# A fused attention and top-1 expert layer: the router's logits by small products from the attention output and the normalised x

## The reference

```python
x = x + tanh(g_xattn) * attention(layernorm(x), ctx, ctx, mask, ...)   # ends in  @ W_o.T + b_o
x = x + tanh(g_ffn) * experts(layernorm(x), gate_w, w1, w2)

def experts(tokens, gate_w, w1, w2):
    gate_logits = tokens @ gate_w.T                  # 2048 x 16
    probs = softmax(gate_logits)
    top1 = argmax(gate_logits)
    mask = one_hot(top1)
    ranks = cumsum(mask, axis=0) - 1
    mask = mask * (ranks < capacity)                 # capacity 160
    ...                                              # every token's row goes to its expert's place
    h = gelu(dispatch @ w1);  expert_out = h @ w2
    out = probs of the chosen expert * expert_out, back in the token's place
```

## Time and profile before

| | |
|---|---|
| median of 3 runs | 346.85 us (345.79 to 347.67) |
| the profiled execution, its own time | 344.49 us |
| its span | 342.7 us |
| TensorE busy | 313.1 us (91%) |
| VectorE busy | 203.1 us (59%) |
| ScalarE busy | 172.8 us (50%) |
| GpSimd busy | 148.6 us (43%) |
| granted TensorE clock, mean | 0.984 |

### The profile page before, as it was taken

How to read it: one execution, slowest core, us unless ns; L and a number is a source line. 1 busy time by engine, 2 the same in 40 slices (tenths; PEclk the granted TensorE clock), 3 DMA queues, 4 the chain that set the end, 5 groups by cost and what they waited for, 6 DMA issues and landing times.

```text
span 342.7 us, 8453 instructions
## 1 busy us (share of the span) xinstructions
PE 313.1 (91%) x2820; PEld 250.7 (73%) x2820; DVE 203.1 (59%) x974; ACT 172.8 (50%) x650; POOL 148.6 (43%) x179
## 2 busy tenths in 40 slices
PE   8868979989989897998879999999999999999990
PEld 4436756876678764886648888888888888888870
DVE  2799788999989895999953333222333333333221
ACT  2489999998999886999302111111111111111110
POOL 6479476676696637665444121222222222111122
PEclk9998999999999999899999999999999999999997
DMA  7911595139621303030053798998988888888300
GB/s 219 297 41 24 197 374 141 26 74 383 215 104 24 95 3 123 7 113 0 2 188 136 215 325 283 292 297 268 275 266 277 271 273 269 261 267 285 130 17 12
DMA packets 42070, 60.54 MB, mean 177 GB/s; under 512 B 3704, under 2 KB 32912, under 8 KB 42032
## 3 DMA queue, kind: packets, MB, share of 16 engines
q1 hardware_dynamic: 38928, 53.28, 49.2%
q0 software_dynamic: 2560, 6.25, 5.1%
q10 hardware_dynamic: 544, 0.52, 0.4%
HBM read 44.60 MB, written 14.19 MB: 172 GB/s over the span
## 4 chain that ended last, share of the span: by engine, by line
PE 60%; DVE 14%; ACT 13%; issue 7%; POOL 3%; POOLq 0%; DVEq 0%
PE bank L1586 20%; PE bank L1603 16%; ACT probs L629 10%; PE bank L1613 4%; DVE probs L827 4%; PE bank L1285 3%; PE bank L1254 2%; DVE rows L894 2%; PE bank L1232 2%; POOL expert_queue L496 2%; DVE probsT L846 2%; PE bank L1193 2%; PE bank L1243 2%; ACT q_par L603 2%; PE bank L1273 1%
## 5 line engine op out<-in xcount | busy, mean ns | idle before, releaser
L629 ACT ACTIVATE probs<-probs,low 128x128 f32<-128x128 f32 x256 | 99.1, 400 | 1.9 <-DVE low L827 1.9
L757 ACT ACTIVATE w_raw<-bank 128x480 f32<-128x480 f32 (+1 forms) x48 | 25.2, 526 | 122.9 <-PE bank L1586 122.9
L480 POOL TENSOR_TENSOR probs<-probs,r_total 128x512 f32<-128x512 f32 x64 | 66.4, 1052 | 31.9 <-DVE r_total L836 31.8
L1586 PE MATMUL bank<-xdT,w 128*128 128x160 f32 x512 | 75.1, 300 | 0.7 <-DVE xdT L1146 0.7
L1586 PEld LDWEIGHTS bank<-xdT,w 128*128 128x128 f32 x512 | 71.6, 190 | 1.7 <-issue 0.9
L1159 DVE SCALAR_TENSOR_TENSOR base<-bank,base 32x256 f32<-32x256 f32 x64 | 30.6, 477 | 65.3 <-PE bank L1613 63.7
L560 POOL DMA_INDIRECT out_dram<-base,place x16 | 15.6, 977 | 116.2 <-DVE base L1167 109.4
L1603 PE MATMUL bank<-w,w_raw 128*128 128x256 f32 x256 | 62.1, 385 | 0.0
L827 DVE CUSTOM_DVE_ANT_0 probs<-bank,mask_now 128x128 f32<-128x128 f32 x256 | 57.3, 284 | 4.4 <-PE bank L1273 4.0
L1603 PEld LDWEIGHTS bank<-w,w_raw 128*128 128x128 f32 x256 | 46.5, 190 | 11.1 <-issue 6.2
L629 ACT ACTIVATION_READ_ACCUMULATOR probs<-probs,low 128x1 f32 x256 | 51.2, 200 | 0.0
(11 more groups left out here) (123 smaller groups left out, 411.1 us busy)
## 6 DMA issues: line engine op xcount, KB each, us to landing
w<-in_L_ffn_w_dram SPq DMA_DIRECT2D x32, 1024.0 KB, 6.2
expert_queue<-empty_row SPq DMA_DIRECT2D x1, 5140.0 KB, 18.2
q_rows<-expert_queue SPq DMA_DIRECT2D x16, 160.0 KB, 6.2
base<-expert_queue SPq DMA_DIRECT2D x16, 129.0 KB, 5.5
ctx_rows<-in_ctx_dram SPq DMA_DIRECT2D x4, 512.0 KB, 10.0
out_dram<-rows SPq DMA_DIRECT2D x4, 512.0 KB, 4.1
x_all<-in_x_dram SPq DMA_DIRECT2D x3, 512.0 KB, 7.2
v_shift<-v SPq DMA_DIRECT2D x12, 128.0 KB, 2.3
```

The source lines that it names most:

```text
L480: pool.tensor_tensor(probs[:, i % NP_], probs[:, i % NP_], r_total[:, i % NP_].unsqueeze(2).to_broadcast([P, PAIRS, 2 * WINDOW]), ALU.mult ...
L629: last = act.activation(probs[:, i % NP_, j], probs[:, i % NP_, j], ACT.Exp, scale=-1.0, bias=low[:, i % NP_, j:j + 1], accum_out=total[:, ...
L757: act.activation(hidden[:, ms[0]:ms[-1] + 1, :], ps_hidden[m][:, 0:n].rearrange("p (m c) -> p m c", c=CAP), ACT.Gelu_apprx_tanh).then_inc( ...
L1586: last = pe.matmul(ps_hidden[m][:, c * CAP:(c + 1) * CAP], w1_sb[i % 2][:, k, f * P:(f + 1) * P], xdT[i % 2][:, k], start=(k == 0), stop=( ...
```

## The change

It uses that layernorm only shifts and scales: x1n times the gate is (x1 times the gate with its row mean taken off) times x1's reciprocal deviation. Maximum and one-hot don't need the positive factor. And x1 is x plus tanh(g) times (attention output times W_o + b_o), so that

- `gate_parts`, once: W_o times the centred gate (`gate_att`, 6 products in all) and b_o times it (`gate_bias`);
- `x_gate`, per batch: the gate times the turned normalised x, 8 products with 32 columns standing, into four strips of ps_wide; `take_x_gate` (VectorE copy 128x128), `x_gate_turn` (one transpose), `x_logits_of` (VectorE, times std, the reciprocal of rstd), `base_logits` (GpSimd adds gate_bias);
- `att_gate` the same with attT and gate_att, `take_att_gate`, `att_gate_turn`, and `sum_logits` (VectorE) the sum of both; `choose` reads that;
- `scale_logits` (GpSimd) multiplies the lowered logits by x1's reciprocal deviation, and `exp_logits` waits for it;
- `x1nT_of`, both `take_x1nT` and `route` of batches 0 to 2 are gone. In the last batch `route` multiplies attT by gate_att directly.

Other things that the same diff moves: a batch's four scatters stand in four places among the norms and reach into the next batch; the last batch's pieces are tiles 0 to 2 and tile 3, x1 of it is made in three parts, and its last eight units go through the windows in another order (both head groups of windows 4, 5 and then of 6, 7), so that tile 2 is complete after chunk 2; expert 0's queued rows are loaded early with batches 0 and 1 alone, and batch 2 goes through `dispatch` too; all 22 `keep_warm` products of the last batch and the tail are gone; W_o is turned later in batch 0; the weights of expert 1 are loaded in batch 2 instead of 1; and the written-out orders of the last batch are new on every engine.

```diff
+            def gate_parts(ps):
+                pe.wait_ge(wT_taken[4], 1)
...
+                for g in range(KD):
+                    for d in range(KD):
+                        pe.matmul(ps[:, g * QUARTER:(g + 1) * QUARTER], w_raw[:, 3, d, g * P:(g + 1) * P], gateT[:, d],
+                                  start=(d == 0), stop=(d == KD - 1))
...
+            def x_gate(n, ps):
...
+                for k in range(KD):
+                    for t in range(T):
+                        last = pe.matmul(ps[t * QUARTER:(t + 1) * QUARTER, 0:P], gateT[:, k], xnT[:, k, t * P:(t + 1) * P],
+                                         start=(k == 0), stop=(k == KD - 1))
+                last.then_inc(x_gate_ready, 1)
...
+            def att_gate_turn(n, ps):
+                pe.wait_ge(att_gate_taken, n + 1)
+                pe.transpose(ps[:, P:2 * P], att_logitsT[:], ident[:]).then_inc(logits_ready, 1)
...
+            def sum_logits(n, ps):
...
+                dve.wait_ge(logits_ready, n + 1)
+                dve.wait_ge(x_logits_based, n + 1)
+                dve.tensor_tensor(logits[:], ps[:, P:2 * P].rearrange("p (t e) -> p t e", e=QUARTER)[:, :, 0:E],
+                                  x_logits[n % 2][:], ALU.add).then_inc(logits_summed, 1)
...
+            def scale_logits(n, m=0):
...
+                pool.tensor_tensor(scaled[:, ts], lowered[:, ts],
+                                   rstd2[:, n % 2, ts].unsqueeze(2).to_broadcast([P, len(tiles(n, m)), E]), ALU.mult
+                                   ).then_inc(scaled_ready, 1)
```

TensorE in batches 1 and 2 (a cut of the diff of the loop over b):

```diff
                 if not first:
                     pe.wait_ge(x1_ready, value(b - 1, 2, 2))
-                    x1nT_of(b - 1, 0)
+                    att_gate(b - 1, ps_wide)
                 pe.wait_ge(xnT_taken, value(b + 1, 2, 1))
                 v_of(b, 1, ps_misc)
+                if not first:
+                    att_gate_turn(b - 1, ps_wide)
+                probsT_of(b, 4)
                 if first:
-                    pe.wait_ge(wT_taken[3], 1)
+                    pe.wait_ge(x_logits_ready, 1)
                 else:
-                    pe.wait_ge(x1nT_taken, value(b - 1, 2, 1))
+                    pe.wait_ge(logits_summed, b)
                 ctxT_of(b + 1, 0, ps_wide)
```

596 lines of the change are left out of this document (354 added, 242 removed).

## The result

The changed kernel took 357.07 us, median of five executions (355.97 to 359.3), the kernel before 347.22 beside it (345.79 to 348.38): ratio 1.0287, 95% interval 1.025 to 1.0324. It is slower by 2.9%. The prediction had 343.3. Run once more, unedited, it took 351.49 us (350.03 to 353.66) against 345.71, ratio 1.0177 (1.0109 to 1.0245). The same program lies 5.6 us apart in the two measurements. The granted clock, a mean over the whole program, goes with the time: 350.03 and 350.7 us at 0.983, 352.28 and 353.66 at 0.966 and 0.964, and 355.97 to 359.3 at 0.962 to 0.949. So there are two losses: 5 to 6 us that stand at a nearly full clock too, and up to 9 more in executions in which TensorE's clock fell. The first profile is of the slowest execution (359.3 us, span 357.6); the second one took 350.7 (span 349.0). Both are read here.

The account below looks back on a forecast made before the run. It took TensorE, ScalarE and VectorE as all full in the attention stage. Terms: -4.1 us at the last exponential (set-up's +1.1 included), +0.6 in the tail, sum -3.5, so 343.3 us from a 346.85 median; range 339.5 to 348.5.

Parts of the forecast that it names:

- I take +1.1 us at the start of batch 1 (bounds 0 and +2).: Set-up in batch 0: gate_parts' matmuls, ScalarE copies and VectorE's small operations delay the start of batch 1 by 1.1 us.
- Batches 1 and 2, 0 each: ScalarE wins 2.0 us a batch from dropped copies and waits; a new stall takes it back; together -3.5 to +4.4.
- The new stall before ctxT: In batches 1 and 2 ctxT_of waits for the summed logits, so ScalarE stalls 2.2 us before copying its result.
- The wait for x_logits: On TensorE attend 1 waits under 1 us for x_logits, hidden by two groups of exponentials already queued.
- So exp 4 starts near 137.3 instead of 140.82: -3.5 us: Last batch: ScalarE's new order of exponentials and copies lets exponential 4 start 3.5 us earlier.
- ScalarE's hole: Idle time of 4.15 us on ScalarE on the way into the last batch, which the new order was to fill.
- The tail, 22.0 us: Last exponential to first expert product: 21.4 us before, 22.0 after, so +0.6 us (bounds -3 and +5).
- slower rival: Tail: VectorE's queue stops at weights_of, behind exponential, scaling, scatters and batch 2's ranks; 349 us, chance 0.13.
- A fall there costs 1.3 to 2 us: Tail without warming matmuls: TensorE waits twice for one-hots, and a clock fall there would leave -2 of the gain.
- the first case's range: The forecast case, 341 to 345.5 us, chance 0.52; the clock falling, at 345, was counted inside it.
- VectorE the bound (0.19): Rival: five added VectorE operations per batch pass through in three batches, taking 3 of 3.5 us; 346.3, no change.
- three signs of being wrong: Granted clock 0.50 after 170; weights_of waiting over 2 us; batch 2's first exponential later than 91.5.

## Why the prediction was wrong

The sum was -3.5 us. At the first expert product the second profile has +6.3, the first +14.9. The forecast had that product at 159.1 + 22.0 = 181.1 us, and the second profile, at a nearly full clock, has it at 190.9. Of these 9.8 us, 0.9 are a later first exponential, 3.5 batch 0, 1.7 batch 1, 3.7 batch 2 up to exponential 4 of the last batch; the two stretches behind that were right together. By its steps:

- **"I take +1.1 us at the start of batch 1 (bounds 0 and +2)."** This failed first. Batch 0 grew by 4.3 to 4.6 us. 2.0 of it is the gate's centring and its transposes ahead of the first v product (shown by moving them). 1.7 lies between its units 8 and 12 and went when W_o was turned earlier, which the q product of batch 1 had waited for (shown too). The rest, 0.6 us at exponential 12 and later, stands where gate_parts does; that it is gate_parts, whose products span 1.4 us on TensorE as estimated, was not tested. I had priced operations and not places: "in a batch where it has room" was wrong for the first exponentials, which wait for VectorE and TensorE. The centring, taken at 0.2, took 2.11.
- **Batches 1 and 2, 0 each.** The new stall before ctxT was right in place and size: 2.20 and 2.71 us for a forecast of 2.2. The wait for x_logits was taken at "under 1 us", hidden; it was 1.57 and 0.87. Not foreseen was the second k product's wait for the rank (1.52), since the rank comes later on VectorE. Batch 1 took +1.7 us, inside the upper bound of 4.4 for both; batch 2, with the way into the last one, -0.9. Shortening the waits, all in one run, gave 0.2 us in batch 1 and 1.2 in batch 2, where about 1.5 a batch was expected, so other work stands close behind them; which, was not separated. How the 1.7 of batch 1 divides between VectorE's added time and its stretched operations stays open; both are of the right size by themselves.
- **"So exp 4 starts near 137.3 instead of 140.82: -3.5 us", and the last exponential "ends at 159.1".** These 3.5 us have the set-up's 1.1 taken off already, so the order was priced at 4.6. In the kernel before it gave 1.0 with a fall of the clock in it and, with the scatters spread, 2.7 without one; 1.2 of either went back to TensorE. In the changed kernel it was 0.9 at exponential 4 and 1.2 at the last one, at a full clock. The step that failed is that ScalarE's hole was taken as the only thing in the way of exponential 4. Two things of the second profile make up the 3.7 us. Exponential 0 came 1.5 us later, from batch 2's start on, than the forecast had it, most of it between units 8 and 12, where ScalarE waits 2.71 us for ctxT. And the copy of q ended 8.5 us behind exponential 0 and not 6.5: ScalarE waited 0.50 us for the k product and 1.16 for low 2, as on VectorE the rank of the batch before, x1 and its statistics stand ahead of low 2. Scores 1 waits for that copy. The 2.2 us from q to exponential 4 were right (2.4). The stretch behind exponential 4, 21.8 us by the sum of groups and copies, was right (22.1).
- **The tail, 22.0 us.** The number was right at a full clock: 21.6 us. The sum walked along VectorE's queue, but the chain that ended last is the slower rival's (scatters, scaled logits, the router's exponential, weights_of). Its price is small, since VectorE's queue is nearly as long: VectorE waits 1.04 us for it in the second profile, and 0.27 to 0.29 in four kernels with warming products and the same tail. The terms were not tested one by one, so that they add up to the right number may be partly luck.
- **The clock, "A fall there costs 1.3 to 2 us".** The mechanism was named and its size was off by a factor of two: 3.8 us (25.4 against 21.6 us, the same tail in two kernels), and 3.6 in the kernel before. Only the waits for one-hots were counted; dispatch of batch 2, called hidden, stands on the path once it runs at half speed (3.26 us). That such a fall is "inside the first case's range" was wrong.
- **VectorE the bound (0.19).** Nearer to what happened in batches 1 and 2 than the forecast, but it had no change for the whole (346.3), and its 0.6 us a batch were too few for batch 1.

Of the three signs of being wrong that were named, batch 2's first exponential later than 91.5 was there in both profiles (96.0 and 97.0), a clock of 0.50 after 170 in the first alone, and a wait of weights_of over 2 us in neither.

## What to carry to other kernels

When three engines are full, a filled hole on one of them is worth what the next engine lets through: price the next wait behind it before counting the hole. Price a small operation by where it stands and by what GpSimd does at that time; 0.3 us of VectorE can become 2.1 beside a long GpSimd operation. And treat warming products as part of the tail's time: whoever adds waits to a stretch of TensorE and takes the products away at once may pay 3 to 4 us in some executions. Where TensorE is full they cost time themselves (1.2 us in the last batch). Before a difference between two profiles is put down to an edit, the granted clock of the stretch has to be compared: here it made 1.3 of 1.6 us that looked like the scatters' gain.

## What the runs showed of the hardware

- With the same wait of 2.00 us on TensorE ahead of the same product, the granted clock behind it was 0.50 in one run and 1.00 in another. Executions of one program differed by 3.6 us, with mean clocks of 0.983 and 0.964. 21 products of 0.2 us brought them within 0.5 us in that kernel, and in three others with such products they still lay 3.4 to 4.7 us apart.
- A half clock costs nothing where TensorE is not waited for: batch 0 with and without it has exponential 4 at 28.91 and 28.92.
- Some of VectorE's operations on SBUF alone (a tensor_scalar, an addition) ended within 0.15 us of GpSimd's running one: 2.11 us for 0.34 and 2.08 for 0.19, both beside one of 2.35 us. A reciprocal at the same place took 0.55 us, against 0.52 elsewhere.
- One execution had two waits on VectorE that lasted 2.5 and 2.1 us beyond the end of what released them. What they are stays open.
